# One transformer block with split fp16 products on one core: a ring of two slots for silu's float outputs, the third weight matrix staged elsewhere, and a new order around the loop

## Chip, core and metric

The kernel runs on one core of one Trainium2 chip. The metric is the device time of one execution in microseconds (us), measured on the slowest core, which here is the only one. The median of three timed executions stands for a kernel, and one further execution is taken with the profiler on.

## The reference

The input x has 16 sequences of 1024 rows with 256 features. The block is a single attention head followed by a gated feed-forward network, each between two layer norms and each with its residual:

```python
def attn(x, W_qkv, b_qkv):                      # d = 256
    qkv = x @ W_qkv.T + b_qkv
    Q, K, V = qkv[..., :256], qkv[..., 256:512], qkv[..., 512:]
    return softmax(Q @ K.T / sqrt(256)) @ V

def ffn(x, wg, wu, wd):                         # int weights, scale 1/127, hidden 768
    return (silu(x @ wg.T) * (x @ wu.T)) @ wd.T

x = x + layernorm(attn(layernorm(x)))
x = x + layernorm(ffn(layernorm(x)))
```

All of it is float32 in the reference.

## The kernel before

**Numbers.** Each operand of a product is split into a high and a low half in fp16 (`xh`, `xl`; `Ph`, `Pl`; `yh`, `yl`; `hTh`, `hTl`). A product is then the sum of two or three fp16 matmuls over 128x128 weights and 256 or 512 columns. ScalarE rounds the high half (an `ACT.Copy` to fp16), GpSimd or VectorE subtracts it from the float value to get the low half. Operands that must have the other axis on partitions are turned by transposing DMAs, all of them issued on SyncE's queue.

**Work of one sequence b.** `x_stats`, `x_norm`, `x_hat`, `x_high`, `x_low` normalise and split x in two halves g of 512 rows. `z_part` projects x by the product of the query and key matrices. From sequence 2 on the scores are formed by a seven-product scheme on pairs of row tiles (`pair_first`, `pair_second`, `pair_third`, `pair_last`), for which `mix_keys` and `mix_queries` form sums and `t_high`, `t_low`, `q_high`, `q_low` split them. `exp`, `p_high`, `p_low` and `turn_p` make the turned probabilities, `attend_part` multiplies them with x, and `project_v` with the value matrix. `y_scale`, `y_stats`, `y_norm`, `x1_add`, `x1_norm`, `y_hat`, `y_high`, `y_low` and `turn_y` make the input of the feed-forward part. There `gate_up` runs eight matmuls of 512 columns for each of six hidden chunks c (four for the gate, four for up), and

- `silu` (ScalarE, L651) writes silu of the gate into a slot of the float tile `hf`,
- `h_mul` (VectorE, L1001) multiplies it with up, in place, or into PSUM for c = 2 and 5 (`HL_ON_VECTOR`),
- `h_high` (ScalarE, L658) rounds it, and `h_low` (GpSimd, L485) or, for c = 2 and 5, `h_rest` (VectorE, L1010) takes the rest.

`hf` has three slots: chunk n (counted over the whole run) uses slot n % 3, and `silu` waits until chunk n - 3 has left its slot, that is for `h_low` of that chunk, or for `h_mul` where the rest is taken from PSUM. `down` multiplies the six chunks with the third weight matrix, and `d_stats`, `d_norm`, `d_add`, `add_bias`, `store` finish the sequence.

**Order.** Nothing decides the order at run time. Each of the five engines has a list of calls, written out for the start, for a loop over b = 1 to 12 and for the end. In one turn of the loop an engine works on up to four sequences at once: the feed-forward part of b, attention of b + 1, scores of b + 2 and the input of b + 3. Semaphores in each helper hold the lists together, and a call whose wait has not ended holds up everything behind it on its engine. PSUM has eight banks, of which 0 to 3, 6 and 7 serve scores, gates and attention in turn, and 4 and 5 take `project_v` and `down`.

**Start.** The first sequence is normalised into `X[2]` and a spare tile and turned on TensorE (`x_first_turn`). `first_z` projects it in three kinds of passes: kind 0 needs the high halves and the high part of the matrix, `A_high`; kinds 1 and 2 need the low ones. The three integer weight matrices are loaded (`load_ffn`), scanned for their size (`ffn_max`), scaled to fp16 halves in staging tiles (`ffn_high`, `ffn_low`) and turned into place (`turn_ffn`). The third one is staged in `hf`. TensorE waits for all three before the first gate.

## Time and profile before

| | us |
|---|---|
| three timed executions | 1324.62, 1324.28, 1322.99 (median 1324.28) |
| profiled execution, its own time | 1322.73 |
| its span, first to last instruction | 1320.9 |
| TensorE matmul busy | 1308.1 (99%) |
| ScalarE / GpSimd / VectorE busy | 1019.5 / 997.6 / 953.1 |

The views used below come from that one execution. A matmul row's duration includes the time until its result is out, so matmuls overlap and the busy time of TensorE hides short pauses. These are read from the distance between the starts of neighbouring matmuls. "Idle before" is the time in which the engine did nothing ahead of an instruction, with what ended it. Positions are us from the start of the span.

### The profile page before, as it was taken

The numbers are of one execution on the slowest core, as the hardware profiler recorded it, in microseconds if no ns is written. First come the engines' busy times: TensorE is split into PE (matmuls) and PEld (weight loads), VectorE is DVE, ScalarE is ACT, GpSimd is POOL, SyncE is SP. The second block draws the span as 40 slices with busy tenths as digits, with TensorE's granted clock in tenths as the row PEclk, the third lists the DMA queues.
The fourth block names the chain that finished last, engine by engine and source line by source line (L and its number), as shares of the span: only waits on it lengthen the run. The fifth ranks groups of instructions, "written<-read, shape, count | busy, mean of one in ns | idle before, by whom it ended". The sixth has DMA issues, their size and how long they took to land.

```text
span 1320.9 us, 23123 instructions
## 1 busy us (share of the span) xinstructions
PE 1308.1 (99%) x7204; PEld 705.6 (53%) x7204; DVE 953.1 (72%) x2670; ACT 1019.5 (77%) x1610; POOL 997.6 (76%) x1081
## 2 busy tenths in 40 slices
PE   8999999999999999999999999999999999999998
PEld 5455455555555555455554555545555555555655
DVE  7877686776867768687686867767687686766566
ACT  6768787788878788787887877878777887867655
POOL 4887687786868868687786877878778686875645
PEclk9999999999999999999999999999999999999999
DMA  6887657676656865578666776666767666666422
GB/s 203 158 172 143 147 93 145 130 153 116 120 124 134 167 119 112 122 138 161 125 115 124 130 148 128 142 124 111 144 128 158 116 119 121 136 132 130 92 64 65
DMA packets 492110, 171.96 MB, mean 130 GB/s; under 512 B 473041, under 2 KB 475473, under 8 KB 491986
## 3 DMA queue, kind: packets, MB, share of 16 engines
q1 hardware_dynamic: 491184, 169.67, 65.1%
q8 instruction: 59, 0.97, 0.3%
q10 hardware_dynamic: 802, 0.79, 0.2%
q14 instruction: 65, 0.53, 0.1%
HBM read 36.70 MB, written 16.78 MB: 40 GB/s over the span
## 4 chain that ended last, share of the span: by engine, by line
PE 90%; POOL 3%; issue 2%; ACT 2%; DMA 2%; SPq 1%; DVE 1%; POOLq 0%; ACTq 0%; DVEq 0%
PE S L1073 71%; PE S L1232 17%; POOL Pl L449 1%; DMA yTl<-yl 1%; SPq L309 1%; DMA PTh<-Ph 1%; POOL qTl L426 0%; POOL yl L476 0%; PE S L1102 0%; PE S L1155 0%; ACT xh L558 0%; SPq L278 0%; ACT P L614 0%; SPq L321 0%; POOL xl L401 0%
## 5 line engine op out<-in xcount | busy, mean ns | idle before, releaser
L449 POOL TENSOR_TENSOR Pl<-P,Ph 128x1024 f16<-128x1024 f32 x128 | 271.4, 2131 | 52.4 <-issue 37.8
L1073 PE MATMUL S<-PTh,xh 128*128 128x512 f16 x512 | 194.1, 379 | 0.0
L1073 PE MATMUL S<-PTl,xh 128*128 128x512 f16 x512 | 194.0, 379 | 0.0
L1073 PE MATMUL S<-PTh,xl 128*128 128x512 f16 x512 | 194.0, 379 | 0.0
L651 ACT ACTIVATE hf<-S,sc 128x512 f32<-128x512 f32 x192 | 129.3, 684 | 64.8 <-PE S L1073 52.8
L614 ACT ACTIVATE P<-P,nmx,sc 128x1024 f32<-128x1024 f32 x112 | 138.2, 1234 | 43.4 <-DVE nmx L901 43.2
L1073 PE MATMUL S<-Wh,hTh 128*128 128x256 f16 x768 | 170.2, 273 | 0.4 <-DVE X L986 0.4
L1073 PE MATMUL S<-Wh,hTl 128*128 128x256 f16 x768 | 170.2, 273 | 0.0
L364 POOL TENSOR_TENSOR rs<-rs,mhalf 128x4 f32<-128x4 f32 (+2 forms) x160 | 146.0, 912 | 13.3
L485 POOL TENSOR_TENSOR hTl<-hf,hTh 128x512 f16<-128x512 f32 x128 | 146.8, 1157 | 8.6 <-ACT hTh L658 5.6
L895 DVE CUSTOM_DVE_ANT_0 P<-S,P 128x512 f32<-128x512 f32 x112 | 76.9, 689 | 96.7 <-ACT P L581 46.6
L1073 PE MATMUL S<-yTh,Gh 128*128 128x512 f16 x384 | 145.6, 379 | 0.8 <-DMA yTl<-yl 0.6
L1073 PE MATMUL S<-yTl,Gh 128*128 128x512 f16 x384 | 145.5, 379 | 0.0
L1073 PE MATMUL S<-yTh,Uh 128*128 128x512 f16 x384 | 145.5, 379 | 0.0
L1073 PE MATMUL S<-yTl,Uh 128*128 128x512 f16 x384 | 145.5, 379 | 0.0
L621 ACT ACTIVATE Ph<-P 128x1024 f16<-128x1024 f32 x128 | 131.1, 1049 | 10.2 <-DMA PTh<-Ph 10.0
L895 DVE CUSTOM_DVE_ANT_0 P<-S,P,mxh 128x512 f32<-128x512 f32 x112 | 83.9, 749 | 53.6 <-PE S L1232 48.3
L1001 DVE SCALAR_TENSOR_TENSOR hf<-S,sc,hf 128x512 f32<-128x512 f32 x128 | 95.1, 745 | 24.7 <-PE S L1073 17.8
L360 POOL TENSOR_SCALAR rs<-mv,sc 128x2 f32<-128x2 f32 (+2 forms) x96 | 30.6, 319 | 78.1 <-DVE mv L977 64.9
L476 POOL TENSOR_TENSOR yl<-yn,yh 128x1024 f16<-128x1024 f32 x32 | 68.3, 2133 | 23.6 <-ACT yh L641 23.6
L1073 PEld LDWEIGHTS S<-Wh,hTh 128*128 128x128 f16 x768 | 75.1, 98 | 16.9 <-issue 4.6
L964 DVE SCALAR_TENSOR_TENSOR S<-S,rinv,bvb 128x256 f32<-128x256 f32 x128 | 53.5, 485 | 40.5 <-PE S L1073 40.5
(206 smaller groups left out, 3295.6 us busy)
## 6 DMA issues: line engine op xcount, KB each, us to landing
xs<-in_L_attn_t SPq DMA_DIRECT2D x32, 512.0 KB, 4.6
X<-in_L_attn_t SPq DMA_DIRECT2D x32, 512.0 KB, 4.6
out_x<-X SPq DMA_DIRECT2D x62, 256.0 KB, 2.9
PTh<-Ph SPq DMA_TRANSPOSE x128, 3.7
PTl<-Pl SPq DMA_TRANSPOSE x128, 3.3
hTh<-in_L_ffn_w_up SPq DMA_DIRECT2D x1, 768.0 KB, 6.9
hTl<-in_L_ffn_w_down SPq DMA_DIRECT2D x1, 768.0 KB, 8.4
hTl<-in_L_ffn_w_gate SPq DMA_DIRECT2D x1, 768.0 KB, 9.8
```

The source lines that it names most:

```text
L364: return p.engine.tensor_tensor(out=rs, in0=rs, in1=mhalf[:, 0:rs.shape[1]], op=ALU.pow)
L449: p.engine.tensor_tensor(out=Pl[:, m % 3, :], in0=P[:, m % 4, :], in1=Ph[:, m % 3, :], op=ALU.subtract).then_inc(pl_vector if i in PL_ON_V ...
L476: p.engine.tensor_tensor(out=yl[:, :, :], in0=yn[:, :, :], in1=yh[:, :, :], op=ALU.subtract).then_inc(yl_done, 1)
L485: p.engine.tensor_tensor(out=hTl[g][:, c, :], in0=hf[:, n % 3, :], in1=hTh[g][:, c, :], op=ALU.subtract).then_inc(hl_vector if c in HL_ON_ ...
L614: a.engine.activation(P[:, m % 4, :], ps[:, bank:bank + 2, :].rearrange("p a n -> p (a n)") if b < 2 else P[:, m % 4, :], ACT.Exp, bias=nm ...
L621: a.engine.activation(Ph[:, m % 3, :], P[:, m % 4, :], ACT.Copy).then_inc(ph_done, 1)
L651: a.engine.activation(hf[:, n % 3, :], ps[:, bank, :], ACT.Silu, scale=sc2[:, 3:4]).then_inc(silu_done, 1)
L895: return v.engine.tensor_tensor_reduce(out=out, in0=ps[:, bank, :], in1=other, scale=1.0, scalar=least, op0=ALU.add, op1=ALU.max, accum_ou ...
L964: v.engine.scalar_tensor_tensor(out=y_tile(t), in0=y_tile(t), scalar=rinv[:, b % 2, 4 * g + t:4 * g + t + 1], in1=bvb[:, :], op0=ALU.mult, ...
L1001: v.engine.scalar_tensor_tensor(out=ps[:, bank + 1, :] if c in HL_ON_VECTOR else hf[:, n % 3, :], in0=ps[:, bank + 1, :], scalar=sc2[:, 4: ...
L1073: done = t.engine.matmul(out, s, m, start=(start and i == 0), stop=(stop and i == len(terms) - 1))
L1232: done = t.engine.matmul(cols(ps[:, bank, :]), s, mv, start=not onto, stop=True, skip_group_check=True)
```

## The change

1. `hf` has two slots. `silu` of chunk n waits for chunk n - 2 to leave its slot.
2. The third weight matrix is staged in `hTh[0]` (high) and in `tTh` (low) instead of in `hf`. So `h_high` of the very first chunk and the turning of `t`'s high half wait for that matrix to be turned, and its `ffn_low` waits for the bias that lay in `tTh` to have been used.
3. The lists of all five engines are rewritten at the start, in the loop and at the end. The number of calls is the same. The loop now begins at another point of the cycle (at the fifth gate of a sequence and no longer in its attention), which alone moves nothing.

```diff
-        hf = sb("hf", [128, 3, 512])
+        hf = sb("hf", [128, 2, 512])
...
-                 (half_words(hf, 3072)[:, 0:1536], half_words(hf, 3072)[:, 1536:3072]))
+                 (half_words(hTh[0], 1536), tTh[:, :, :, :].rearrange("p a b n -> p (a b n)")[:, 0:1536]))
...
-            if low:
-                s.wait_ge(ffn_turned[1], 32)
+            s.wait_ge(ffn_turned[1 if low else 2], 32)
...
-            if n > 2 and (n - 3) % 6 in HL_ON_VECTOR:
-                a.wait_ge(hmul_done, n - 2)
-            elif n > 2:
-                hl_wait(a, (n - 3) // 6, (n - 3) % 6)
-            a.engine.activation(hf[:, n % 3, :], ps[:, bank, :], ACT.Silu, scale=sc2[:, 3:4]).then_inc(silu_done, 1)
+            if n > 1 and (n - 2) % 6 in HL_ON_VECTOR:
+                a.wait_ge(hmul_done, n - 1)
+            elif n > 1:
+                hl_wait(a, (n - 2) // 6, (n - 2) % 6)
+            a.engine.activation(hf[:, n % 2, :], ps[:, bank, :], ACT.Silu, scale=sc2[:, 3:4]).then_inc(silu_done, 1)
...
+            if n == 0:
+                a.wait_ge(ffn_turned[2], 32)
...
+            if n == 2:
+                v.wait_ge(bv_ready, 1)
```

`h_high`, `h_low` and `h_mul` index `hf` by n % 2 in the same way. In the start of SyncE's list the load of the second half of sequence 1 moves ahead of the three weight loads:

```diff
             load_x(s, 1, 0)
+            load_x(s, 1, 1)
+            load_ffn(s, 2)
+            load_ffn(s, 0)
             load_ffn(s, 1)
-            load_ffn(s, 2)
-            load_x(s, 1, 1)
-            load_ffn(s, 0)
+            load_x(s, 2, 0)
             turn_x(s, 1, 0, 0)
-            load_x(s, 2, 0)
```

At the entry into the feed-forward part of sequence 0, `h_high(a, 0, 0, 1)` moves in ScalarE's list from behind the fourth silu to a place ahead of `y_high(a, 0, 1)` and the third silu. At the end of TensorE's list the last pairs read so:

```diff
-            pair_first(t, 15, 3, (u3_copied, 55), (c11_done, 55), (c12_done, 55), (c21_done, 55))
             project_v(t, 14, 1, (x1_done, 114), (x1_done, 116))
+            pair_first(t, 15, 3, (u3_copied, 55), (c11_done, 55), (c12_done, 55), (c21_done, 55))
             pair_second(t, 15, 3)
+            gate_up(t, 14, 0, 0, 6, (ol_done[0], 30), (ol_done[1], 30), three)
             pair_third(t, 15, 3)
-            gate_up(t, 14, 0, 0, 6, (ol_done[0], 30), (ol_done[1], 30), three)
-            gate_up(t, 14, 0, 1, 0, (u3_copied, 56), (c11_done, 56), three)
             down(t, 13, 1, 0, (x1_done, 118), three)
+            down(t, 13, 1, 1, (x1_done, 120), three)
             pair_last(t, 15, 3)
-            down(t, 13, 1, 1, (x1_done, 120), three)
+            gate_up(t, 14, 0, 1, 0, (u3_copied, 56), (c11_done, 56), three)
```

**ScalarE at the start.** The rows run from the first normalised tiles of sequence 0 (`X`, `tTl`) to its first projection (`zTh`); `Ah` is `A_high`, `xTh` a turned high half. Before:

```order
L538 ACTIVATE X<-xs,nb,rs 128x256 x2
L538 ACTIVATE tTl<-xs,nb,rs 128x256 x2
L543 ACTIVATE xTh<-S 128x4x128
L521 ACTIVATE Ah<-S,sc 128x512
L543 ACTIVATE xTh<-S 128x4x128
L538 ACTIVATE tTl<-xs,nb,rs 128x256 x2
L558 ACTIVATE xh<-X 128x1024
L543 ACTIVATE xTh<-S 128x4x128 x2
L570 ACTIVATE zTh<-S,cb 128x512 x2
```

and in the changed kernel:

```order
L537 ACTIVATE X<-xs,nb,rs 128x256 x2
L537 ACTIVATE tTl<-xs,nb,rs 128x256 x4
L520 ACTIVATE Ah<-S,sc 128x512
L542 ACTIVATE xTh<-S 128x4x128 x2
L557 ACTIVATE xh<-X 128x1024
L569 ACTIVATE zTh<-S,cb 128x512 x2
L542 ACTIVATE xTh<-S 128x4x128 x2
```

The last two normalised tiles now stand ahead of `Ah` and of both turned halves that the first projection needs, and the second half's turned pieces stand behind `zTh`.

**VectorE at the start**, from the low part of the matrix to the low halves of z (`zTl`); `st<-xs` are the statistics of an input half. Before:

```order
L739 SCALAR_TENSOR_TENSOR xTl<-S,xTh 128x4x128
L768 SCALAR_TENSOR_TENSOR Al<-S,sc,Ah 128x512
L739 SCALAR_TENSOR_TENSOR xTl<-S,xTh 128x4x128
L826 BN_STATS st<-xs 128x6 x4
L830 BN_AGGR mv<-st 128x2 x4
L837 TENSOR_SCALAR zw<-S,cb 128x512 x2
L739 SCALAR_TENSOR_TENSOR xTl<-S,xTh 128x4x128 x2
L409 TENSOR_TENSOR zTl<-zw,zTh 128x512 x2
```

and in the changed kernel:

```order
L769 SCALAR_TENSOR_TENSOR Al<-S,sc,Ah 128x512
L740 SCALAR_TENSOR_TENSOR xTl<-S,xTh 128x4x128 x2
L829 BN_STATS st<-xs 128x6 x4
L833 BN_AGGR mv<-st 128x2 x4
L829 BN_STATS st<-xs 128x6 x4
L833 BN_AGGR mv<-st 128x2 x4
L840 TENSOR_SCALAR zw<-S,cb 128x512 x2
L740 SCALAR_TENSOR_TENSOR xTl<-S,xTh 128x4x128 x2
L408 TENSOR_TENSOR zTl<-zw,zTh 128x512 x2
```

The statistics of the second half of sequence 1 now stand ahead of `zw`, the float copy of the first projection.

**GpSimd in the loop**, from `x1_norm` of the second half (`nb`) into the first chunks of the feed-forward part; `tl`, `yl`, `hTl` are the low halves of t, y and h. Before:

```order
L369 TENSOR_SCALAR nb<-nb 128x4
L485 TENSOR_TENSOR hTl<-hf,hTh 128x512
L418 TENSOR_TENSOR tl<-xs,th 128x1024
L476 TENSOR_TENSOR yl<-yn,yh 128x1024
L485 TENSOR_TENSOR hTl<-hf,hTh 128x512
L360 TENSOR_SCALAR rs<-mv,sc 128x2
```

and in the changed kernel:

```order
L368 TENSOR_SCALAR nb<-nb 128x4
L417 TENSOR_TENSOR tl<-xs,th 128x1024
L484 TENSOR_TENSOR hTl<-hf,hTh 128x512 x2
L475 TENSOR_TENSOR yl<-yn,yh 128x1024
L359 TENSOR_SCALAR rs<-mv,sc 128x2
```

Both `hTl`, the ones that free the two slots, now stand ahead of `yl`.

## Rows read from the trace of the kernel before

**Rows 1.** The page: busy time of each engine, and TensorE's granted clock in 40 slices.

```profile
PE 1308.1 (99%) x7204; PEld 705.6 (53%) x7204; DVE 953.1 (72%) x2670; ACT 1019.5 (77%) x1610; POOL 997.6 (76%) x1081
...
PEclk9999999999999999999999999999999999999999
```

**Rows 2.** The chain that ended last, in time: start us, us, what.

```profile
498.04 33.36 PE S L1073 x202
...
578.51 33.41 PE S L1073 x202
...
659.65 33.36 PE S L1073 x202
```

**Rows 3.** Timeline of TensorE: start us, us, instruction, [idle before <-releaser].

```profile
657.10 0.39 PE L1073 MATMUL S<-yTh,Gh 128*128 128x512 f16 x1 [0.45 <-DMA yTl<-yl]
```

**Rows 4.** Timeline of ScalarE from 11.9 to 14.5 us.

```profile
11.97 0.60 ACT L543 ACTIVATE xTh<-S 128x512 f16<-128x512 f32 x1
12.46 0.68 ACT L521 ACTIVATE Ah<-S,sc 128x512 f16<-128x512 f32 x1
13.03 0.60 ACT L543 ACTIVATE xTh<-S 128x512 f16<-128x512 f32 x1
13.51 1.10 ACT L538 ACTIVATE tTl<-xs,nb,rs 128x256 f32<-128x256 f32 x2
```

**Rows 5.** Timeline of TensorE: the first projection and the first scores.

```profile
13.20 1.09 PE L1155 MATMUL S<-xTh,Ah 128*128 128x512 f16 x4 [0.37 <-ACT Ah L521]
...
17.60 0.38 PE L1189 MATMUL S<-xTh,zTh 128*128 128x512 f16 x1 [0.71 <-ACT zTh L570]
...
19.33 1.03 PE L1155 MATMUL S<-xTh,Ah 128*128 128x512 f16 x4
```

**Rows 6.** Timeline of VectorE: statistics of sequence 1, and the float copy of z.

```profile
15.29 1.40 DVE L826 BATCH_NORM_STATS2 st<-xs 128x6 f32<-128x256 f32 x4 [0.27 <-DMA xs<-in_L_attn_t]
16.61 0.36 DVE L830 BATCH_NORM_AGGREGATE mv<-st 128x2 f32<-128x6 f32 x4
17.49 1.41 DVE L837 TENSOR_SCALAR zw<-S,cb 128x512 f32<-128x512 f32 x2 [0.52 <-ACT zTh L570]
```

**Rows 7.** Timeline of SyncE's queue: the two loads of sequence 1.

```profile
10.71 0.33 SPq L267 DMA_DIRECT2D xs<-in_L_attn_t  x1
...
14.63 0.34 SPq L267 DMA_DIRECT2D xs<-in_L_attn_t  x1
```

**Rows 8.** DMA issues: count, KB each, median us from issue to landing.

```profile
xs<-in_L_attn_t SPq DMA_DIRECT2D x32, 512.0 KB, 4.6
...
yTl<-yl SPq DMA_TRANSPOSE x32, 3.2
```

**Rows 9.** Timeline of ScalarE: entry into the feed-forward part of sequence 0.

```profile
104.18 0.62 ACT L658 ACTIVATE hTh<-hf 128x512 f16<-128x512 f32 x1
...
105.65 1.26 ACT L651 ACTIVATE hf<-S,sc 128x512 f32<-128x512 f32 x2
```

**Rows 10.** Timeline of TensorE at the same place.

```profile
106.52 0.38 PE L1073 MATMUL S<-yTl,Uh 128*128 128x512 f16 x1
107.05 0.38 PE L1073 MATMUL S<-xTh,Ah 128*128 128x512 f16 x1
```

**Rows 11.** The waits: who waited for whom, us in total, times, longest.

```profile
ACT hf L651 <- POOL hTl L485: 11.7, 19, 1.5
```

**Rows 12.** Timeline of GpSimd in the turn that begins at 740.12 us.

```profile
750.13 2.13 POOL L476 TENSOR_TENSOR yl<-yn,yh 128x1024 f16<-128x1024 f32 x1 [0.22 <-ACT yh L641]
752.22 1.16 POOL L485 TENSOR_TENSOR hTl<-hf,hTh 128x512 f16<-128x512 f32 x1
```

**Rows 13.** Timeline of TensorE in that turn: the first gate matmul of the second half.

```profile
756.48 0.38 PE L1073 MATMUL S<-yTh,Gh 128*128 128x512 f16 x1
```

**Rows 14.** Timeline of TensorE near the end.

```profile
1218.63 0.39 PE L1232 MATMUL S<-tTh,qTh 128*128 128x512 f16 x1 [0.69 <-ACT P L587]
...
1223.33 0.27 PE L1073 MATMUL S<-Wh,hTh 128*128 128x256 f16 x1 [0.42 <-DVE X L986]
```

More of the change, by code:

```diff
@@ L484, in h_low @@
             p.wait_ge(dn_done[1], 2 * (b - 1) + g + 1)
-            p.engine.tensor_tensor(out=hTl[g][:, c, :], in0=hf[:, n % 3, :], in1=hTh[g][:, c, :], op=ALU.subtract
+            p.engine.tensor_tensor(out=hTl[g][:, c, :], in0=hf[:, n % 2, :], in1=hTh[g][:, c, :], op=ALU.subtract
                                    ).then_inc(hl_vector if c in HL_ON_VECTOR else hl_done, 1)
@@ L657, in h_high @@
             a.wait_ge(dn_done[1], 2 * (b - 1) + g + 1)
-            a.engine.activation(hTh[g][:, c, :], hf[:, n % 3, :] if bank is None else ps[:, bank + 1, :], ACT.Copy).then_inc(hh_done, 1)
+            if n == 0:
+                a.wait_ge(ffn_turned[2], 32)
+            a.engine.activation(hTh[g][:, c, :], hf[:, n % 2, :] if bank is None else ps[:, bank + 1, :], ACT.Copy).then_inc(hh_done, 1)
         def add_bias(a, b, g, pair):
@@ L1808, in _ @@
[L1808 to L1812 removed]
+            x_high(a, 3, 0)
+            silu(a, 0, 1, 4, 6)
+            h_high(a, 0, 1, 2, 0)
+            h_high(a, 0, 1, 3)
+            add_bias(a, 0, 0, 0)
+            h_high(a, 0, 1, 4)
+            silu(a, 0, 1, 5, 2)
+            h_high(a, 0, 1, 5, 2)
+            copy_m1(a, 2, 0)
+            p_high(a, 1, 6)
+            p_high(a, 1, 7)
@@ L2043, in _ @@
             silu(a, 15, 0, 1, 0)
-            silu(a, 15, 0, 2, 2)
+            h_high(a, 15, 0, 0)
+            h_high(a, 15, 0, 1)
             y_hat(a, 15, 1, 0)
@@ new lines, in second_part @@
+            attend_part(t, 1, 1, 5)
+            attend_part(t, 1, 1, 1)
+            pair_third(t, 2, 2)
+            attend_part(t, 1, 1, 7)
+            attend_part(t, 1, 1, 3)
+            pair_last(t, 2, 2)
+            pair_first(t, 2, 3, (u3_copied, 3), (c11_done, 3), (c12_done, 3), (c21_done, 3))
+            project_v(t, 1, 1, (x1_done, 10), (x1_done, 12))
+            pair_second(t, 2, 3)
+            z_part(t, 3, 0, 0, 6, (ol_done[0], 4))
+            pair_third(t, 2, 3)
+            z_part(t, 3, 0, 1, 7, (ol_done[1], 4))
@@ L2476, in second_part @@
+            gate_up(t, 1, 0, 0, 0, (u3_copied, 4), (c11_done, 4), three)
+            pair_last(t, 2, 3)
+            down(t, 0, 1, 0, (x1_done, 14), three)
+            down(t, 0, 1, 1, (x1_done, 16), three)
+            gate_up(t, 1, 0, 1, 2, (c12_done, 4), (c21_done, 4), three)
+            gate_up(t, 1, 0, 2, 0, (silu_done, 13), (hmul_done, 13), three)
+            gate_up(t, 1, 0, 3, 2, (silu_done, 14), (hmul_done, 14), three)
+            for b in range(1, 13):
                 gate_up(t, b, 0, 4, 6, (mix_z, 10 * b + 4), (mix_z, 10 * b + 5), three)
@@ L2521, in second_part @@
-            pair_third(t, 14, 3)
-            z_part(t, 15, 0, 1, 7, (ol_done[1], 28))
-            gate_up(t, 13, 0, 0, 0, (u3_copied, 52), (c11_done, 52), three)
-            pair_last(t, 14, 3)
-            down(t, 12, 1, 0, (x1_done, 110), three)
-            down(t, 12, 1, 1, (x1_done, 112), three)
-            gate_up(t, 13, 0, 1, 2, (c12_done, 52), (c21_done, 52), three)
-            gate_up(t, 13, 0, 2, 0, (silu_done, 157), (hmul_done, 157), three)
-            gate_up(t, 13, 0, 3, 2, (silu_done, 158), (hmul_done, 158), three)
+                attend_part(t, b + 1, 1, 2)
@@ new lines, in second_part @@
+                pair_third(t, b + 2, 2)
+                attend_part(t, b + 1, 1, 7)
+                attend_part(t, b + 1, 1, 1)
+                attend_part(t, b + 1, 1, 3)
+                pair_last(t, b + 2, 2)
+                pair_first(t, b + 2, 3, (u3_copied, 4 * b + 3), (c11_done, 4 * b + 3), (c12_done, 4 * b + 3), (c21_done, 4 * b + 3))
+                project_v(t, b + 1, 1, (x1_done, 8 * b + 10), (x1_done, 8 * b + 12))
+                pair_second(t, b + 2, 3)
+                z_part(t, b + 3, 0, 0, 6, (ol_done[0], 2 * b + 4))
@@ new lines, in second_part @@
+                pair_third(t, b + 2, 3)
+                z_part(t, b + 3, 0, 1, 7, (ol_done[1], 2 * b + 4))
+                gate_up(t, b + 1, 0, 0, 0, (u3_copied, 4 * b + 4), (c11_done, 4 * b + 4), three)
+                pair_last(t, b + 2, 3)
+                down(t, b, 1, 0, (x1_done, 8 * b + 14), three)
+                down(t, b, 1, 1, (x1_done, 8 * b + 16), three)
+                gate_up(t, b + 1, 0, 1, 2, (c12_done, 4 * b + 4), (c21_done, 4 * b + 4), three)
+                gate_up(t, b + 1, 0, 2, 0, (silu_done, 12 * b + 13), (hmul_done, 12 * b + 13), three)
@@ L2576, in second_part @@
+            down(t, 13, 1, 1, (x1_done, 120), three)
+            pair_last(t, 15, 3)
             gate_up(t, 14, 0, 1, 0, (u3_copied, 56), (c11_done, 56), three)
-            down(t, 13, 1, 0, (x1_done, 118), three)
-            pair_last(t, 15, 3)
-            down(t, 13, 1, 1, (x1_done, 120), three)
             gate_up(t, 14, 0, 2, 2, (c12_done, 56), (c21_done, 56), three)
```

894 lines of the change are left out of this document (428 added, 466 removed).

## The prediction

> **What bounds the kernel now.** I read the page first. TensorE is busy for 1308.1 of 1320.9 us, the other engines for 72 to 77% each, and TensorE's granted clock is 9 tenths or more in all 40 slices [rows 1]. So only TensorE's own pauses can be won, and the next question is how many there are. The busy time cannot tell, since a matmul row lasts 0.38 us while neighbours start 0.216 us apart (eight from 17.60 to 19.33 us [rows 5]). I therefore went to the chain of waits in order of time. It runs through TensorE turn after turn of the loop, and the same place of the cycle comes back at 498.04, 578.51 and 659.65 us: one turn of 80.47 us and one of 81.14 us [rows 2]. The work itself: one turn holds 372 matmuls of 512 columns, or what corresponds to them in pairs of 256 (96 for attention, 24 for z, 84 for scores, 24 for the value product, 96 for gates, 48 for down). 372 times 0.216 us is 80.35 us. The faster turn is at that floor, so in most turns nothing can be gained, however the lists stand. The slower one has a pause at 657.10 us, where the first gate matmul of a sequence waits for the turned low half of y [rows 3].
>
> Then I went through the distances between matmul starts over the whole span. Behind the first 14 us there are few pauses over 0.1 us. The larger ones: 0.7 us ahead of the first scores [rows 5], 0.3 us at 107.05 us [rows 10], 0.6 us at 657.10, and two of 0.7 and 0.4 us idle near the end [rows 14]. All pauses together are some 5 us. That is the most that a better order can win. An order that makes TensorE wait anywhere loses without such a limit.
>
> **The change, part by part.** Work is the same in kind and number: no instruction is added beyond waits, so the sum is of pauses of TensorE alone.
>
> *Start, ScalarE.* The first projection needs `A_high` and the first turned half. ScalarE did them from 11.97 to 13.63 us, and the two normalised tiles came behind, at 13.51 us for 1.10 us [rows 4]. TensorE began the projection at 13.20 us, just released by `A_high` [rows 5]. Now the two tiles come first. They take the 1.0 us (1.10 less the 0.1 by which neighbouring ScalarE rows overlap) ahead of `A_high`: tiles until 12.8, `A_high` until 13.4, the first turned half until 13.9 us. The projection begins at 13.95 instead of 13.20 us: **0.75 us later**. TensorE turns the second half of x behind it as before, which is ready earlier but is not waited for at that point. The first scores wait for z anyway and move along, from 17.60 to 18.35 us. All of TensorE's work is still ahead, so nothing hides this.
>
> *Start, VectorE.* The load of the second half of sequence 1 waits for the two tiles. It went out at 14.63 us, and goes out at about 12.9 us now, ahead of the weights [rows 7]. At 4.6 us from issue to landing [rows 8] it is there at 17.5 us. Its statistics take 1.7 us, as the first half's did from 15.29 to 16.97 us [rows 6], so until 19.15 us, and `zw` with its 1.41 us now stands behind them: done at 20.5 us. Before it was done at 18.90 us [rows 6]. The projection of the second half needs its bank. It began at 19.33 us [rows 5], behind eight score matmuls, and would be ready at 18.35 + 1.73 = 20.08 us. So TensorE pauses for another **0.45 us**. Bounds: nothing if the load lands by 17.0 us, and 1.4 us if the weight loads behind it hold it up by another 1 us. I take 0.45, from the median of the 32 loads.
>
> *The third weight matrix.* Its halves leave `hf` for `hTh` and `tTh`. The new waits are for a matrix that TensorE waits for in any case before its first gate, and the bias is used by the same product whose result scales them. I cost this part at nothing: the cover is that wait ahead of the gates. Were the matrix late, the first gate would be late with it, in both kernels.
>
> *Entry into the feed-forward part.* At 107.05 us the projection into bank 2 waits 0.31 us (0.53 us between starts instead of 0.216) for the fourth silu, which ends at 105.65 + 1.26 = 106.91 us [rows 9, 10]. One more rounding of h, 0.62 us less the overlap of 0.1, now stands ahead of it in ScalarE's list [rows 9]. The chain ahead of it is unbroken ScalarE work. So it costs **0.5 us**.
>
> *Ring of two in the loop.* Already with three slots silu waited for GpSimd's `hTl` 19 times, 11.7 us in all and 1.5 us at most, without TensorE standing still [rows 11]: between a silu and the gate that takes its bank lie 1.7 to 3.5 us of other matmuls. With two slots each silu needs the `hTl` of one chunk later. The new list brings those forward, and pays with `yl`. Before, `yl` of the second half ran at 750.13 us for 2.13 us, and `hTl` of chunk 1 (1.16 us) behind it [rows 12]. Now that `hTl` stands ahead. Of the 1.16 us, 0.22 us was idle time [rows 12], so `yl` ends up to 0.94 us later, at 753.2 instead of 752.26 us. It is turned in 3.2 us [rows 8], so it lands at 756.4 us, and the first gate matmul of the second half wants it at 756.48 us [rows 13]. The margin shrinks from 1.0 to about 0.1 us, in each of twelve turns. Below, the cost is nothing. Above, I take 0.5 us a turn: the other places with as little room (the last `hTl` by VectorE ahead of the next scores, the mixing of queries ahead of the sixth gate) have ScalarE operations of 0.6 to 1.06 us ahead of them, and half of one such operation is what could be missing. As the margin comes out just positive I take the near end, 0.05 us a turn, **0.6 us** in all.
>
> *The pauses for `yl` of the first half* (as at 657.10 us). In the new list ScalarE rounds y of the first half earlier, ahead of a copy of attention's second output and of one exponential. GpSimd is free by then. The turned half then arrives earlier, and what made one turn 0.67 us longer than the next [rows 2] should go: **-0.7 us**.
>
> *End.* `pair_third` followed `pair_second` directly and waited for a copy in between: 0.7 us idle. Two gates further on `down` waited 0.4 us for `x1_add` [rows 14]. The new order puts a gate into the first gap, which removes it. But it runs the value product directly behind the last attention part and only one `pair_last`, while the rounding (0.6 us) and the rest (0.7 us) of that part's output must come in between: about 1 us of new pause. The two cancel within 0.3 us; I take **0**, with 1 us to either side.
>
> Sum: 0.75 + 0.45 + 0.5 + 0.6 - 0.7 = 1.6 us on the profiled execution's 1322.73 us. The median of the timed runs is 1324.28 us, 1.55 us above it, and the same difference set on it gives **1325.9 us**. About 0.2%, 2.65 us, is what a measurement of this kernel can tell from no change.
>
> **The rivals.**
>
> *The ring becomes the bound in the loop (slower).* The place is silu of chunks 2 to 5 behind `hTl` of the chunk two before. The gate that reuses the bank comes 1.7 to 3.5 us after, and from the point at which a silu is later than that, each further us is a us of TensorE, twelve times. For it: with three slots silu was already held up to 1.5 us [rows 11], and the margin of `yl` falls to 0.1 us [rows 13]. Against it: the two `hTl` have moved forward, and TensorE never waited for a silu in the loop. At 0.4 us a turn it gives 4.8 instead of 0.6 us, together 1.6 + 4.2 = 5.8 us: 1330.1 us. The Trainium skill (Perfetto Trace Analysis, Optimization Strategy) says that consistent bubbles, the same gap in each turn on the engine that should be saturated, can mean that there aren't enough buffers. By that rule a ring cut by a third is where such a gap would begin; the trace of before shows none on TensorE, with turns at the floor of the work, so the rule raises this rival's chance and not my sum.
>
> *The start is cheap and the pauses go (faster).* If the load lands by 17.0 us and the end gains both its pauses, with the first half of y never late: 0.75 + 0.5 - 1.3 (the late turns, all of them) - 1.4 (the end) - 1.2 (later pauses up to 107 us that swallow the late start) = -2.7 us: 1321.6 us. For it: those pauses are real. Against it: the pauses before 107 us hang on chains that start from TensorE itself, and shift with it.
>
> *No difference at all.* The late start is taken up by pauses that stand behind it, and the loop has no pause: 1.6 - 0.5 - 0.6 = 0.5 us, 1324.8 us. Here the change is a pure release of memory.
>
> **How the numbers follow.** My forecast has 0.48, the slower rival 0.33, the faster one 0.09, no difference 0.10. The forecast's own range is 1324.3 to 1327.9 us, of which the upper end is over the 0.2% (1326.9 us): I count 0.05 of its 0.48 as slower, and 0.01 as faster. That gives faster 0.1, same 0.52, slower 0.38. The range from 1322.5 to 1331.0 us leaves out the faster rival's centre and a loop that loses over 0.45 us a turn.
>
> **What would show it.** In the profile of the changed kernel: the first projection at about 13.95 us and the second half's at 20.5 us instead of 19.33 us, with an idle time behind `zw`; the pause at 107 us now at about 109 us and near 0.8 us; turns of 80.5 to 80.6 us, and none over 81; `yl` of the second half landing within 0.2 us of the gate that needs it. Wrong would be: turns of 80.9 us or more, with silu waiting for GpSimd well over 11.7 us in total; or the first projection still at 13.2 us.

## Result: 22 us slower, and where they are

The changed kernel takes 1345.87 us (median of 4 runs, 1344.19 to 1348.58), beside 1323.63 us for the kernel before on the same chip (median of 4, 1321.86 to 1324.62). The ratio is 1.0178, with a 95% interval from 1.0166 to 1.0190. Predicted was 1325.9 us, with a range from 1322.5 to 1331.0 us. The profiled execution lasted 1346.91 us, its span 1345.0 us. From its page:

```profile
span 1345.0 us, 23141 instructions
## 1 busy us (share of the span) xinstructions
PE 1314.0 (98%) x7204; PEld 703.3 (52%) x7204; DVE 954.2 (71%) x2670; ACT 1022.8 (76%) x1612; POOL 999.8 (74%) x1081
...
PEclk9999999999999999999999999999999999999999
```

Nothing in it looks worse than [rows 1]: TensorE is busy for 98% and its clock reads 9 tenths in each slice. The 24.2 us by which the two profiled executions differ do not show there. They show in the distances between matmul starts, and in four stretches of the program that begin and end at the same matmul in both kernels, the first gate matmul (`S<-yTh,Gh`) of a sequence:

| stretch, us | before | changed | difference |
|---|---|---|---|
| start to first gate of sequence 0 | 96.75 | 105.19 | +8.4 |
| to first gate of sequence 1 | 76.38 | 77.13 | +0.8 |
| to first gate of sequence 13 (12 turns) | 967.41 | 978.96 | +11.5 |
| to the last instruction | 180.31 | 183.76 | +3.5 |

The waits of TensorE name the largest part at once. The columns are the engine, the line, who was waited for, us in total, times, longest. Changed kernel:

```profile
PE S L1235 <- ACT P L586: 9.0, 8, 1.5
PE S L1076 <- DMA yTl<-yl: 2.9, 4, 1.3
PE S L1076 <- issue: 2.9, 1, 2.9
...
PE S L1158 <- ACT xTh L542: 1.6, 1, 1.6
PE S L1076 <- DMA PTl<-Pl: 1.3, 1, 1.3
PE S L1076 <- DVE oTl L955: 1.0, 1, 1.0
```

L586 is `copy_u2`, by which ScalarE takes the second partial sum of a pair of scores out of the accumulator, so that `pair_third` can go on. Eight of the twelve turns have such a wait. The kernel before has none of that size in its loop. The silus, on which I had put the risk, waited for GpSimd's `hTl` 26 times and 11.1 us in all, no longer than the 11.7 us of [rows 11].

**The loop's pause, followed back.** Timelines of ScalarE, TensorE and SyncE's queue in the turn of 737 us, changed kernel (start us, us, engine, instruction, [idle before <-releaser]):

```profile
732.02 0.57 ACT L580 ACTIVATE P<-S 128x512 f32<-128x512 f32 x1
736.27 1.06 ACT L620 ACTIVATE Ph<-P 128x1024 f16<-128x1024 f32 x1 [3.67 <-DMA PTl<-Pl]
737.23 0.58 ACT L586 ACTIVATE P<-S 128x512 f32<-128x512 f32 x1
...
737.86 0.39 PE L1235 MATMUL S<-tTh,qTh 128*128 128x512 f16 x1 [1.04 <-ACT P L586]
```
```profile
723.89 0.58 SPq L320 DMA_DIRECT2D out_x<-X  x1
724.51 2.66 SPq L278 DMA_TRANSPOSE xTh<-xh  x1
727.21 0.57 SPq L320 DMA_DIRECT2D out_x<-X  x1
730.19 0.34 SPq L297 DMA_DIRECT2D X<-in_L_attn_t  x1
730.58 1.24 SPq L308 DMA_TRANSPOSE PTh<-Ph  x1
731.86 2.41 SPq L308 DMA_TRANSPOSE PTl<-Pl  x1
```

TensorE waits for `copy_u2`. That copy stands behind a rounding (`p_high`, L620) in ScalarE's list, and the rounding had waited 3.67 us until its buffer, the one of exponential 0, was turned. That turn (`PTl`, issued at 731.86 us) landed at 736.18 us. This rounding waited so in all twelve turns, 39.9 us in total; in the eight turns in which TensorE paused it waited 3.4 to 4.2 us, in the other four 2.3 to 2.6 us. The turn stood on SyncE behind the reload of X (L297), and the reload waits until the store of the same buffer has landed: the store went out at 727.21 us, and SyncE issued nothing until 730.19 us. In the list the store, the reload and the two turns now follow one another. SyncE's own waits (us in total, times, longest) show the same thing over the whole span, first changed, then before:

```profile
SPq L297 <- DMA out_x<-X: 33.6, 14, 3.5
```
```profile
SPq L298 <- DMA out_x<-X: 9.5, 4, 2.6
```

Twelve of the fourteen waits are the first reload of each turn, 2.3 to 3.5 us each. In the kernel before none of the four lies in the loop.

**The start.** The first projection began at 14.12 us, as forecast (13.95). What the forecast lacks is the clock behind that pause. Stretches of time, changed kernel (stretch, length, busy time and number of instructions of each engine, granted clock, DMA share, GB/s):

```profile
12.00:14.00 2.00, 0.53 (x5) 0.44 (x4) 0.57 (x2) 2.00 (x5) 0.00 (x0) 0.89 0.76 254
14.00:16.00 2.00, 1.88 (x6) 0.88 (x7) 2.00 (x5) 1.41 (x2) 0.51 (x1) 0.50 0.67 166
16.00:18.00 2.00, 2.00 (x12) 1.62 (x12) 1.19 (x7) 0.00 (x0) 1.83 (x3) 0.76 0.90 270
36.00:38.00 2.00, 1.62 (x7) 0.78 (x8) 1.96 (x4) 0.30 (x1) 0.00 (x0) 0.86 0.00 0
38.00:40.00 2.00, 2.00 (x6) 0.65 (x5) 1.97 (x6) 2.00 (x4) 0.00 (x0) 0.50 0.00 0
```

The clock falls to its lower level, 1.2 GHz (0.50), and matmuls of 512 columns start 0.427 us apart instead of 0.216. At 14 us eleven matmuls begin at that level (four of 512 columns, and seven in float32 of 128 columns, 0.213 us apart instead of 0.109), and from the first projection to the first scores 5.72 us pass instead of 4.40. Behind 37 us it is eight of 512 columns, 1.7 us. Together 3.0 us are lost so.

The second place is a pause of 3.06 us that ends at 36.38 us. Timelines of VectorE, GpSimd and TensorE, changed kernel:

```profile
29.82 1.40 DVE L840 TENSOR_SCALAR zw<-S,cb 128x512 f32<-128x512 f32 x2
31.13 5.15 DVE L408 TENSOR_TENSOR zTl<-zw,zTh 128x512 f16<-128x512 f32 x2
...
31.08 2.13 POOL L448 TENSOR_TENSOR Pl<-P,Ph 128x1024 f16<-128x1024 f32 x1 [1.69 <-ACT Ph L620]
33.17 2.56 POOL L400 TENSOR_TENSOR xl<-xs,xh 128x1024 f16<-128x1024 f32 x1
...
36.38 0.38 PE L1076 MATMUL S<-xTh,zTh 128*128 128x512 f16 x1 [2.90 <-issue]
```

The score matmuls need the low half of the second z. In the new list VectorE makes it behind two row maxima and `ffn_max`, as GpSimd works on its own differences. The two operations take 5.15 us, where they took 1.28 us before (25.66 us, beside small operations of GpSimd). TensorE goes on 0.1 us after they end.

Up to the turned maxima at 51.11 us (43.59 before) these parts add up: 0.9 us for the later projection, 1.3 for the clock, 0.5 for `zw`, 3.1 for the second z and 1.7 for the clock behind it are 7.5 us. The rest of the 8.4 us are a pause of 0.40 us at 55.08 us and one of 0.61 us for `yTl` ahead of the first gate.

**The end.** Three pauses of over 0.8 us are new: ahead of the value product (1.12 us between starts beyond the normal distance, idle 0.96 us for `oTl`), ahead of the first gate of sequence 14 (0.86, for `yTl`), and ahead of the last attention parts (1.44, for `PTl`), besides two of 0.64 us. The kernel before has 0.85 and 0.59 us there, of which [rows 14] show 0.69 and 0.42 us as idle time. The second one of 0.64 us is a gate's:

```profile
1306.13 0.39 PE L1076 MATMUL S<-yTh,Uh 128*128 128x512 f16 x1 [0.47 <-DVE hTl L1013]
```

### The profile page after: what moved, and what is told of

It is laid out like the page before. It is cut to its first block and busy times, and to the rows that moved or that the text cites. A ratio compares the mean times of both kernels' runs of the same rounds, so it can differ in the third digit from the quotient of the medians.

```text
span 1345.0 us, 23141 instructions
## 1 busy us (share of the span) xinstructions
PE 1314.0 (98%) x7204; PEld 703.3 (52%) x7204; DVE 954.2 (71%) x2670; ACT 1022.8 (76%) x1612; POOL 999.8 (74%) x1081
## 5 line engine op out<-in xcount | busy, mean ns | idle before, releaser
L620 ACT ACTIVATE Ph<-P 128x1024 f16<-128x1024 f32 x128 | 132.7, 1048 | 42.1 <-DMA PTl<-Pl 39.9
L1004 DVE SCALAR_TENSOR_TENSOR S<-S,sc,hf 128x512 f32<-128x512 f32 x64 | 48.5, 758 | 64.8 <-ACT hf L650 55.2
L659 ACT ACTIVATE hTh<-hf 128x512 f16<-128x512 f32 x128 | 79.8, 625 | 12.1 <-DVE hf L1004 11.0
```

Source lines behind the costliest of these rows:

```text
L620: a.engine.activation(Ph[:, m % 3, :], P[:, m % 4, :], ACT.Copy).then_inc(ph_done, 1)
L659: a.engine.activation(hTh[g][:, c, :], hf[:, n % 2, :] if bank is None else ps[:, bank + 1, :], ACT.Copy).then_inc(hh_done, 1)
L1004: v.engine.scalar_tensor_tensor(out=ps[:, bank + 1, :] if c in HL_ON_VECTOR else hf[:, n % 2, :], in0=ps[:, bank + 1, :], scalar=sc2[:, 4: ...
```

## Experiments

Each kernel ran on the same chip as runs of the kernel before, whose median was 1322.1 to 1322.4 us. Ratios are to those. Beside the total I give the stretches of the table above, as "first gate" (before 96.75, changed 105.19), "loop" (967.4, 979.0) and "end" (180.3, 183.8), each from one profiled execution.

**The reload moved (SyncE's loop).**

```diff
-                reload(s, b + 1, 0)
                 turn_p(s, b + 2, 1, 0)
                 turn_p(s, b + 2, 0, 1)
+                reload(s, b + 1, 0)
```


> The changed kernel with one row moved in SyncE's loop: the reload of X for the first half goes behind the two turns of the exponentials (1,0) and (0,1), ahead of which it stands. Theory A (a queue held by a round trip): the reload waits until the store of the same buffer, issued just ahead of it, has landed (some 3 us), and holds the two turns behind it; the rounding of exponential 3 waits for the second of them, copy_u2 of pair 2 stands behind that rounding on ScalarE, and TensorE waits for the copy ahead of pair_third. Then the eight pauses of 1.0 to 1.7 us ahead of the product of the turned token weights (11 us together) go, and the kernel takes 1334.5 to 1337.5 us instead of 1345.9. Theory B (the ring of two holds the loop): no pause moves, 1345 to 1347 us. Theory C (ScalarE is too full there in any case): the copy comes late by its own work, less than 3 us gained.

1333.52 us, ratio 1.0089 (1.0076 to 1.0103). The loop takes 968.1 us, all eight pauses are gone, and `PE S L1235 <- ACT P L586` has left the waits. The same place in this kernel, ScalarE and SyncE's queue:

```profile
723.71 1.04 ACT L620 ACTIVATE Ph<-P 128x1024 f16<-128x1024 f32 x1
726.78 0.60 ACT L586 ACTIVATE P<-S 128x512 f32<-128x512 f32 x1 [2.02 <-PE S L1235]
```
```profile
718.99 1.29 SPq L308 DMA_TRANSPOSE PTh<-Ph  x1
720.32 1.33 SPq L308 DMA_TRANSPOSE PTl<-Pl  x1
721.70 0.58 SPq L297 DMA_DIRECT2D X<-in_L_attn_t  x1
```

ScalarE no longer waits for the turn, and the copy now waits for TensorE instead of the reverse. Theory A holds, B and C fall. The total lies 1 us below theory A's range: the first gate came at 100.3 us with the same first lists, 4.9 us earlier than in the changed kernel's profile, and that part of the gain is not the reload's (below).

The queue still stands, only elsewhere. The moved reload waits in none of the twelve turns, but the second reload of each turn, with one row between it and its own store, now waits 1.1 to 3.7 us (in the changed kernel at most 0.1 us):

```profile
723.61 0.58 SPq L320 DMA_DIRECT2D out_x<-X  x1
724.78 1.30 SPq L308 DMA_TRANSPOSE PTh<-Ph  x1
728.10 0.34 SPq L297 DMA_DIRECT2D X<-in_L_attn_t  x1
```
```profile
SPq L297 <- DMA out_x<-X: 27.7, 14, 3.7
```

The loop pays nothing that shows for these 27.7 us. What cost the 10.9 us is which rows stood behind the wait: the rounding's own wait for `PTl` went from 39.9 us in twelve places to 0.7 us in one.

**The copy ahead of the rounding (ScalarE's loop), reload as in the changed kernel.**

```diff
-                p_high(a, b + 2, 3)
                 copy_u2(a, b + 2, 2)
+                p_high(a, b + 2, 3)
```


> The changed kernel with two rows of ScalarE's loop exchanged: copy_u2 of pair 2 stands ahead of the rounding of exponential 3 instead of behind it. SyncE's list stays as it is, so the reload still holds the two turns. If the delay reaches TensorE through that rounding on ScalarE (theory A, as the reload's move suggested), the pauses ahead of pair_third go here too, since the copy no longer stands behind the late turn: 1334 to 1338 us. The turn itself stays late, so what hangs on the exponentials' own halves may pay 1 or 2 us. If TensorE waited for the turned exponentials themselves, or another engine carried the delay, the pauses stay or come back a few matmuls later: 1343 to 1347 us.

1343.91 us, ratio 1.0146 (1.0129 to 1.0164); loop 975.4 us. The pauses ahead of `pair_third` are gone, and pauses of 0.4 to 1.1 us stand ahead of the value product (`S<-Vh,oTh`), in all twelve turns. The delay now takes another way:

```profile
572.29 0.60 ACT L586 ACTIVATE P<-S 128x512 f32<-128x512 f32 x1 [2.97 <-PE S L1235]
573.10 1.06 ACT L620 ACTIVATE Ph<-P 128x1024 f16<-128x1024 f32 x1 [0.21 <-DMA PTl<-Pl]
...
574.29 2.14 POOL L448 TENSOR_TENSOR Pl<-P,Ph 128x1024 f16<-128x1024 f32 x1 [2.16 <-ACT Ph L620]
...
578.47 2.08 ACT L633 ACTIVATE yn<-X,nb,rs 128x256 f32<-128x256 f32 x4 [2.34 <-POOL nb L368]
```

The copy waits for TensorE again, and the rounding behind it begins when copy and turn are both done, which here is nearly the same time. GpSimd's difference follows it and holds up `nb`, ScalarE's `yn` waits for that, and `oTh`, which the value product needs, stands behind `yn`. In all the rounding waited only 1.5 us for `PTl`, in five places; in the other turns the copy ahead of it was done last, so part of this price is the edit's own and not the queue's. Of 11.5 us, 3.5 came back. Theory A was right about the path to `pair_third` and wrong about the price; the total is the one expected for pauses that come back a few matmuls later. This run alone would not show that the queue is the source; the moved reload does.

**Three slots again.** The ring of float h as before, all else as changed (`n % 3`, silu waits for the chunk three before).

> The changed kernel, its order and its staging, with float h in a ring of three slots again. Theory A (the order costs, not the ring): only the single pause of 1.5 us at 772.5 us, where a silu waited for GpSimd, can go, and perhaps 0.5 us at the end: 1343.5 to 1346 us. Theory B (the ring is the bound in the loop, the rival of the prediction): the loop's pauses of some 13 us go, 1331 to 1335 us.

1342.12 us, ratio 1.0144 (1.0128 to 1.0159). The loop takes 978.2 us with its eight waits for the copy (8.6 us), and the pause at 772 us, which I had put down to the ring, is still there with 1.7 us. Theory B falls. The total fell by 1.4 us more than theory A allows, but not in the loop: in the profiled execution, the slowest of its four, the first gate stands at 103.1 us instead of 105.2, with the same first lists and one stretch of lower clock less.

**The same with the reload moved.**

> The changed kernel with the reload moved (1333.5 us), and float h in three slots again. With the loop at the floor of its work, this shows what the ring of two costs by itself. Theory A (the ring costs nothing in the loop): 1332.5 to 1335 us, and the stretch from the first gate of sequence 1 to that of sequence 13 takes 968 us as with two slots. Theory B (my term for the ring, or more): 0.6 to 2 us less in that stretch, 966 to 967.5 us.

1336.07 us, ratio 1.0098 (1.0082 to 1.0113), whose interval overlaps that of two slots. The loop takes 968.3 us, with two slots 968.1, as in theory A, though the total lies 1 us above its range. No silu waits for `hTl` any more, and the loop is no shorter for it: the one pause of 0.33 us that goes (for `hTl`, at 926.39 us) is lost again elsewhere. The end took 182.1 us here and 185.0 us with two slots. But the kernel with three slots above has 184.3 us there, and others with two have 183.4 to 184.7 us. One pause does follow the ring: that for `hTl` ahead of a late gate (0.64 us in the changed kernel) is there with 0.64 to 0.70 us in every kernel with the new order and two slots, and in neither of the two with three. How much more of the end is the ring's stays open.

**Staging alone.** The kernel before, order and ring unchanged, with the third weight matrix staged in `hTh` and `tTh`, and the waits that this needs:

```diff
-                 (half_words(hf, 3072)[:, 0:1536], half_words(hf, 3072)[:, 1536:3072]))
+                 (half_words(hTh[0], 1536), tTh[:, :, :, :].rearrange("p a b n -> p (a b n)")[:, 0:1536]))
```


> The kernel before, its order and its three slots, with only the staging of the third weight matrix moved to hTh and tTh and with the waits that this needs. The prediction costed it at nothing: within 1 us of the kernel before (1321.1 to 1323.1 us). Rival: the rounding of the first h and the turns of t, which now wait for the matrix to be turned, make the first gates late: 1 us or more on top.

1322.16 us (11 runs), ratio 1.0001 (0.9992 to 1.0010). It costs nothing.

**ScalarE's five operations at the start.**

```diff
-            x_first_scalar(a, 6)
-            x_first_scalar(a, 7)
-            A_high(a)
             xT_first_high(a, 0, 4, 0)
+            A_high(a)
             xT_first_high(a, 0, 4, 1)
+            x_first_scalar(a, 6)
+            x_first_scalar(a, 7)
```


> The changed kernel with ScalarE's first list as it was before for five operations: the first turned half, A_high and the second turned half ahead of the two normalised tiles. Theory A: the first projection starts at 13.2 us again instead of 14.1 us, TensorE never idles for 1.85 us, and its granted clock stays at full speed (behind that pause 13 matmuls ran at half of it, some 2 us): 1.5 to 3 us less than the changed kernel, 1343 to 1344.4 us. Theory B: the late load of the second half of sequence 1 and the 3 us pause at 36 us swallow what is won at the start: within 1 us of the changed kernel, though the clock at 14 to 17 us is full again.

1348.15 us, ratio 1.0195 (1.0181 to 1.0209). The first projection began at 12.95 us, with the clock at 1.00 in the two stretches from 12 to 16 us, and nothing was won: the kernel is some 2 us slower than the changed one, by the ratios, where theory B had them within 1 us. The second one began at 21.97 us, behind a pause of 2.9 us, since VectorE's `zw` stands behind statistics whose load, issued at 14.38 us behind the two tiles, landed at 18.9 us. Behind that pause the granted clock was 0.78 and 0.79 in the two stretches from 20 to 28 us, and the pause of 3.06 us for the second z stayed. TensorE's waits:

```profile
PE S L1158 <- DVE zw L840: 2.7, 1, 2.7
```

**VectorE's maxima and second z at the start.**

```diff
-            V_max(v)
-            ffn_max(v, 0)
+            z_float(v, 0, 1, 2)
             row_max(v, 0, 0, 4)
+            z_low(v, 0, 1)
             row_max(v, 0, 1, 6)
-            z_float(v, 0, 1, 2)
-            z_low(v, 0, 1)
             row_max(v, 0, 2, 0)
+            V_max(v)
+            ffn_max(v, 0)
```


> The changed kernel with VectorE's first list as it was before: the float z of the second half of sequence 0 and its low half go back ahead of the row maxima, and V_max and ffn_max(0) behind the third. Theory A: the pause of 3.06 us at 36.38 us is the low half of z (5.15 us for two operations that take 0.68 us each when GpSimd rests) directly ahead of scores that need it; moved forward it is late for nobody even if it takes 5 us, and the half clock behind the pause goes too (nine matmuls at 0.427 instead of 0.216 us, 1.9 us): 4 to 5 us less than the changed kernel, 1341 to 1342 us. Theory B: the maxima are what is late (ffn_max ahead of them), and the pause shrinks by less than 1.5 us or comes back at the next scores: 1344 us or more.

1345.31 us, ratio 1.0178 (1.0163 to 1.0192). The pause at 36 us went, as in theory A, and one of 2.12 us appeared at 45.81 us, ahead of scores that wait for an exponential to leave their bank: `ffn_max(1)`, `ffn_max(2)` and the statistics of sequence 2 still stand ahead of that exponential's maximum, `row_max(0, 4)`. The first gate came at 101.7 us instead of 105.2 in the profiled execution, the fastest of its five, but the median says theory B: no gain.

**Both of these, the statistics behind z again, and the reload moved.**

> The changed kernel with the reload moved (1333.5 us) and both first lists back: ScalarE's five operations, and on VectorE the statistics of the second half of sequence 1 behind the low half of z, the second z ahead of the maxima, V_max and ffn_max(0) behind the third. Theory A (the two lists hold each other's gain back: ScalarE's order alone only moved the wait to the load of the second half of sequence 1 on VectorE, 18.9 us; VectorE's alone left the late first projection): the first gate falls from 100.3 us to 97 to 98 us, 1328.5 to 1331.5 us. Theory B (the loads behind, in another order on SyncE, are what is late): the first gate stays at 99 us or later, 1332 us or more.

1336.77 us, ratio 1.0105 (1.0089 to 1.0120), first gate 104.6 us. Theory A falls, by over 5 us. Total and first gate are as in theory B, but no wait here is for the loads that it named. The pause behind the maxima had grown to 2.86 us:

```profile
46.76 0.61 PE L1076 MATMUL S<-xTh,zTh 128*128 128x512 f16 x1 [2.70 <-ACT P L613]
```

It is the wait of the run before, for the exponential whose maximum stands behind `ffn_max(1)` and `ffn_max(2)`. Three more, of 0.44 to 0.85 us, stand ahead of it: ScalarE's `x_hat(1, 1)` still stood ahead of `z_high`, and now waited 2.06 us for the later statistics. The clock fell twice, at 12.6 and at 46.7 us. The rows moved here only handed the wait on.

**The first lists of four engines as before, and the reload moved.** ScalarE's rows up to the second silu of sequence 0, VectorE's up to maximum 6 of sequence 1, GpSimd's up to its fourth `h_low` and SyncE's up to the turn of exponential 4, in the order of before.

> The changed kernel with the reload moved, and with the first lists of all four engines in the order of before: ScalarE up to the second silu of sequence 0, VectorE up to the maximum 6 of sequence 1, GpSimd up to the fourth rounding rest of h, SyncE up to the turn of exponential 4. Theory A (the start costs 4 to 8 us, and no single row does it: a row moved alone meets the next row that waits for the same late load, as the start of the runs before showed): the first gate of sequence 0 at 96.7 to 97.5 us instead of 100 to 105 us, and 1328 to 1330 us, what is left being the end. Theory B (the rest of SyncE's first list, which stays changed, is what is late): first gate at 99 us or later, 1331 us or more.

1341.14 us, ratio 1.0140 (1.0124 to 1.0155). Up to 43.67 us TensorE is where it was before (the turned maxima begin at 43.59 us there, at 51.11 us in the changed kernel): the first 7.5 us are the order of these lists. Behind the cut nearly all was given back, in three pauses of 1.7, 2.5 and 3.8 us, at 52.50, 75.76 and 116.52 us; behind the last two the clock fell again (0.50 from 78 to 80 and from 118 to 120 us). The rows there, the rest of SyncE's among them, are still the new ones and were written for other neighbours; which of them are late this run does not separate. So theory A falls; the numbers are those of theory B, whose cause is not shown. The first gate came at 102.8 us. The last of the three shows what a ring of two can do in an order that is not made for it, ScalarE and TensorE:

```profile
115.68 0.69 ACT L650 ACTIVATE hf<-S,sc 128x512 f32<-128x512 f32 x1 [2.83 <-POOL hTl L484]
...
116.52 0.38 PE L1076 MATMUL S<-xTh,Ah 128*128 128x512 f16 x1 [3.61 <-ACT hf L650]
```

GpSimd does the 2.12 us of `yl` ahead of `hTl` there, the silu waits for that, and TensorE for the silu.

**An exponential ahead of the first silu at the end, and the reload moved.**

```diff
-            silu(a, 14, 0, 0, 6)
             exp(a, 15, 6)
+            silu(a, 14, 0, 0, 6)
```


> The changed kernel with the reload moved (1333.5 us) and, behind the loop, the exponential 6 of sequence 15 ahead of the first silu of sequence 14 instead of behind it. Theory A: between the two silus it costs ScalarE two table loads of 1.28 us that the kernel before has not; without them what stands behind on ScalarE comes 2.5 us earlier, and the pauses at the end shrink by what hangs on ScalarE: the 1.3 us ahead of the first gate of sequence 14 no (it waits for the turned low half of y), the 1.7 us ahead of the last attention parts yes. 1332 to 1333 us. Theory B: ScalarE has room at the end, and the last turn is late through GpSimd and SyncE alone: no difference, 1333 to 1334 us.

1339.30 us, ratio 1.0121 (1.0105 to 1.0136). It is worse: the end takes 187.7 us instead of 185.0 (most of the rest of the difference is the start's, 105.2 us against 100.3). The two table loads are saved (32 instead of 34), but the exponential waits for its maximum, and the silu behind it with it:

```profile
1237.46 1.24 ACT L613 ACTIVATE P<-P,nmx,sc 128x1024 f32<-128x1024 f32 x1 [1.46 <-DVE nmx L904]
...
1238.81 1.28 ACT L650 ACT_TABLE_LOAD   x1
```

A pause of 2.5 us appears at 1243.39 us. Both theories fall: the changed order pays two table loads of 1.28 us, and a wait of this kind would be the alternative.

**Two edits at the end, on top of the first lists.**

```diff
-            project_v(t, 14, 1, (x1_done, 114), (x1_done, 116))
             pair_first(t, 15, 3, ...)
+            project_v(t, 14, 1, (x1_done, 114), (x1_done, 116))
...
-            turn_p(s, 15, 7, 1)
-            turn_p(s, 15, 7, 0)
             turn_p(s, 15, 6, 1)
+            turn_p(s, 15, 7, 0)
+            turn_p(s, 15, 7, 1)
```


> The kernel of the run before (first lists of before, reload moved) with two edits behind the loop: the value product of sequence 14 stands behind pair_first of pair 3 again, and on SyncE the turn of the low half of exponential 6 of sequence 15, ready some 2 us before it is issued, goes ahead of the two turns of exponential 7. Theory A: the pause of 1.12 us ahead of the value product goes, and of the 1.4 to 2.0 us ahead of the last attention parts some 1.3 us: 2 to 2.4 us less than the run before, 1326 to 1328 us. Theory B (behind each pause another operand is late by as much): under 1 us less.

1340.09 us, ratio 1.0134 (1.0118 to 1.0149). The turn did its part: the pause ahead of the last attention parts fell from 1.88 to 0.38 us. The value product did not: its pause went, one of 0.88 us came ahead of the scores, and one of 2.77 us ahead of `down`, which waits for the residual formed from that product:

```profile
1235.47 0.27 PE L1076 MATMUL S<-Wh,hTh 128*128 128x256 f16 x1 [2.61 <-DVE X L989]
```

Theory B, for one edit of the two: the end takes 185.6 us, 1.0 us more than in the run before, and the two medians, 1 us apart, do not tell the kernels apart. No run here has the whole of SyncE's first list in the order of before, so what it would give back stays open. Only the staging alone is as fast as the kernel before.

## Why the prediction was wrong

- **SyncE's queue (the step that failed; 10.9 of the profile's 24.2 us).** My part on the loop went through ScalarE's and GpSimd's lists and gave the loop 0.6 us and -0.7 us. I never asked what each row of SyncE's list is queued behind. The new list puts a reload directly behind the store that it waits for, and the turns of the exponentials behind the reload. The moved row shows it: 979.0 us against 968.1 for the loop.
- **The ring of two (rival, 0.33).** It gave 4.8 us and named silu behind `hTl`. It is not what happened: with the reload moved, the loop takes 968.1 us with two slots and 968.3 with three, before 967.4. What remains against before is 0.7 us in twelve turns. My term of 0.6 us comes near it by luck: it was 0.05 us in each turn for a `yl` that is barely late, and what the profile with the reload moved shows is one pause of 1.38 us, with three slots 1.41 us. The ring's own pause is the 0.64 to 0.70 us at the end, where I had put none. The sign that I had set for this rival, "turns of 80.9 us or more", did come (81.6 us a turn) from a mechanism that neither side had. The other half of it, silus waiting well over 11.7 us, did not (11.1 us), and that half told the rivals apart.
- **Staging: 0.** Right (1.0001).
- **ScalarE at the start: +0.75.** Right in place, 14.12 instead of 13.20 us. But I took later work to move along at its old speed. With the pause of 1.85 us the clock fell, and the eleven matmuls at the lower level cost 1.3 us more.
- **VectorE at the start: +0.45.** The pause measured 0.52 us, near by luck, since two errors cancel. I took the page's median of 4.6 us for the load; it took 6.1 us and landed at 19.0 us, 1.5 us later than I had it. But TensorE, at the lower clock, was ready for the second projection only at 21.57 us, also 1.5 us later. So the projection began at 22.09 instead of 20.5 us. Where the first projection came on time, in the run with ScalarE's five operations back, the pause was 2.89 us.
- **Left out: VectorE's list from 23 to 45 us.** I costed the edits ahead of the second projection and stopped. Behind it stand the second z next to GpSimd's operations (3.06 us, and 1.7 us at the lower clock) and the maxima behind `ffn_max`, which cost 2.12 us once the first was gone. With the two above, the start costs 8.4 us where I had 1.2.
- **Entry into the feed-forward part: +0.5.** The pause is 0.49 us (0.31 before), in other kernels with this order 0.83; the stretch to the first gate of sequence 1 costs 0.8 us. Near enough.
- **The pauses for `yl` of the first half: -0.7.** In the loop they did go, three of 0.28 to 0.61 us before, one of 0.26 us now; outside it they came up at the first gates of sequences 0 and 14 (0.61 and 0.86 us). `yl` of the second half, whose margin I saw shrink to 0.1 us, was late once, 1.5 us at 772.51 us.
- **End: 0, with 1 us to either side.** The value product directly behind the attention part costs 1.12 us, as forecast, and the gap that goes gave 0.85. The turned exponentials (1.44 us) and the turned `yl` (0.86 us) I had not looked at; for the first, the moved turn shows SyncE's queue again. The stretch costs 3.5 us.
- **"Work is the same in kind and number".** Not quite: ScalarE has two table loads more (34 instead of 32), at the end, 1.28 us each. The run without them was slower, so no gain of theirs shows.

The rule of the Trainium skill that I had weighed (Perfetto Trace Analysis, Optimization Strategy: the same gap in each turn can mean too few buffers) met its case in eight turns of twelve, and no buffer was short: the third slot left all eight where they were. A repeated gap says that a cause lies in the cycle, and not which.

What stays open: why the rounding waits up to 2 us longer in some turns than in others, though each has the same lists (TensorE pauses only in the eight with 3.4 us or more); which rows of the lists behind 44 us cost what is left of the start; and what makes `yl` of the second half late in one turn.

## What to carry to other kernels

Ask of every row of a DMA queue what it waits for and what stands behind it. Here a reload directly behind the store of its buffer held the queue for 2.3 to 3.5 us in every turn, and cost TensorE 10.9 us in the loop while the turns of two exponentials stood behind it. With those two turns ahead the loop was back near the floor, though the queue then stood for 24 us in all at the other reload (30 us before the move). The bill came two engines away, in a wait that names the wrong one. Where whole lists were reordered, most of the single moves tried here only handed the wait on to the next row; the move that paid took a cause out of the cycle.

## Unexpected on the chip

**VectorE and GpSimd exclude each other in some operations.** One of VectorE's `zTl` operations takes 0.68 us. When the first of a pair started at 31.13 us, 0.05 us after GpSimd's difference, the pair took 5.15 us: each of the two ended 0.5 us after the GpSimd operation beside it (33.21 and 35.73 us). In the kernel with the reload moved VectorE was first by a hair, and GpSimd's operation grew from 2.13 to 2.66 us instead, and the pair took 3.22 us:

```profile
30.55 3.22 DVE L408 TENSOR_TENSOR zTl<-zw,zTh 128x512 f16<-128x512 f32 x2
...
30.55 2.66 POOL L448 TENSOR_TENSOR Pl<-P,Ph 128x1024 f16<-128x1024 f32 x1 [1.22 <-ACT Ph L620]
```

The Trainium skill (SBUF — State Buffer, SBUF: two separate sides) has it as a lock on the port pair that the two engines share, for VectorE's operations with two inputs in SBUF among others, as these are: whoever starts first holds it for its whole instruction. The trace agrees in both orders. TensorE's pause was 3.06 us in the one and 1.13 us in the other, with the same lists. In the six profiled kernels that share these first lists the first gate comes between 100.3 and 105.2 us. Most of that is this race (1.13 us of pause in one, 3.06 in the other five) and the clock behind the pause, so totals of these kernels that differ by less than 3 us say little without the stretches.

**The clock.** With the first pause of 1.85 us the granted clock fell to 0.50. Behind 0.77 us it stayed at 1.00 in the run with ScalarE's five operations back, behind 1.26 us also in the run with the first lists, but in the run with both starts, behind 0.76 us, it was 0.65 and then 0.50. The pause of 3.06 us for the second z is the same in five kernels with these first lists, and in three of them the clock fell behind it (0.50 from 38 to 40 us in the changed kernel), in the two with three slots it did not (1.00 from 36 to 40 us in both), nor in the run with ScalarE's five operations back, which has the same pause (1.00 from 36 to 42 us). Each such stretch costs 1.3 to 1.7 us here. A late start costs more than its wait, and not the same each time.
